# The new projection together with gate and up products between the routing steps, and the router on four column tiles

## The reference

```python
x = x + tanh(g_xattn[0]) * xattn(layernorm(x), ctx, ctx, Wq, bq, Wk, bk, Wv, bv, Wo, bo)   # 16 heads of 16
x = x + tanh(g_ffn[0]) * ffn(layernorm(x), w_router, fc1_w, fc2_w, gate_w, up_w, down_w)

def ffn(h, ...):                                  # h: 2048 x 256
    logits = h @ w_router                         # 256 x 8
    top_logits, top_idx = top_k(logits, 2)
    scores = softmax(top_logits)
    # each token goes through its two experts e:
    proj, gate = split(h @ fc1_w[e], 2)           # 256 x 512
    out_e = silu(proj) * gate @ fc2_w[e]          # 256 x 256
    moe = sum over the two experts of out_e * score
    shared = silu(h @ gate_w) * (h @ up_w) @ down_w   # 256 x 512, 512 x 256
    return moe + shared
```

## Time and profile before

| | |
|---|---|
| time, median of 3 runs | 496.63 us (495.54 to 497.8) |
| time of the profiled execution | 495.35 us |
| its span | 493.6 us, 7811 instructions |
| PE busy | 479.7 us, 97% of the span |
| DVE busy | 318.9 us, 65% |
| ACT busy | 228.9 us, 46% |
| POOL busy | 121.9 us, 25% |
| mean DMA rate | 112 GB/s |

### The profile page before, as it was taken

One profiled execution on the slowest core, in us unless ns is written; L12 is line 12 of the kernel. 1 busy time (PEld: TensorE's weight loads), 2 busy tenths in 40 slices (PEclk: granted clock), 3 DMA queues, 4 the chain that ended last, 5 costly groups with the idle time before them and its releaser, 6 DMA issues.

```text
span 493.6 us, 7811 instructions
## 1 busy us (share of the span) xinstructions
PE 479.7 (97%) x2234; PEld 245.9 (50%) x2235; DVE 318.9 (65%) x775; ACT 228.9 (46%) x487; POOL 121.9 (25%) x139
## 2 busy tenths in 40 slices
PE   8999898999999999999999999999999999999997
PEld 7555332332333323333457666565666666665645
DVE  1887887888888888888567776233333333332574
ACT  2655466777777777777754110032222333321010
POOL 5593483000000000000000757601333333333000
PEclk9999989999999999999999899999999999999999
DMA  8659742799994222220000213512222222221931
GB/s 257 201 176 252 160 152 76 192 194 190 196 191 143 66 65 67 64 66 1 3 2 0 76 64 108 183 38 71 86 89 91 87 85 85 87 74 45 329 122 60
DMA packets 49170, 55.46 MB, mean 112 GB/s; under 512 B 8080, under 2 KB 41232, under 8 KB 49136
## 3 DMA queue, kind: packets, MB, share of 16 engines
q1 hardware_dynamic: 44096, 43.86, 33.6%
q0 software_dynamic: 3408, 9.34, 5.4%
q10 hardware_dynamic: 1632, 1.84, 1.2%
HBM read 35.18 MB, written 19.71 MB: 111 GB/s over the span
## 4 chain that ended last, share of the span: by engine, by line
PE 84%; DMA 6%; DVE 4%; SPq 2%; ACT 1%; issue 1%; POOL 1%; ACTq 0%; POOLq 0%
PE PS L1420 14%; PE PS L1164 11%; PE PS L1331 11%; PE PS L1074 10%; PE PS L1282 10%; PE PS L1409 7%; PE PS L1343 6%; PE PS L1125 3%; PE PS L1212 2%; DMA R<-mparts 2%; PE PS L1174 2%; DMA X<-in_x_dram 2%; DMA q_parts<-R 2%; PE PS L1401 2%; PE PS L1394 2%; PE PS L1233 1%
## 5 line engine op out<-in xcount | busy, mean ns | idle before, releaser
L691 DVE TENSOR_REDUCE nmax<-PS 128x1 f32<-128x512 f32 x256 | 162.1, 682 | 18.5 <-PE PS L1074 17.9
L599 ACT ACTIVATE R<-PS 128x512 f32<-128x512 f32 x256 | 133.7, 603 | 41.9 <-PE PS L1282 41.8
L1074 PE MATMUL PS<-R 96*128 96x512 bf16 x256 | 96.5, 384 | 2.4 <-DMA R<-k_parts 1.6
L1282 PE MATMUL PS<-R 98*128 98x512 bf16 x256 | 86.3, 381 | 3.5 <-DMA R<-mparts 2.4
L1420 PE MATMUL PS<-R 128*128 x156 | 73.6, 594 | 1.5 <-ACT R L651 1.0
L1164 PE MATMUL PS<-R 128*32 128x512 f32 x512 | 68.2, 605 | 0.0
L487 POOL DMA_INDIRECT token_y<-R,dest x39 | 37.4, 959 | 98.9 <-DVE R L983 98.6
L999 DVE TENSOR_TENSOR R<-R,PS 128x256 f32<-128x256 f32 x39 | 16.4, 422 | 67.8 <-ACT R L648 42.2
L1074 PEld LDWEIGHTS PS<-R 96*128 96x128 bf16 x256 | 24.8, 97 | 58.2 <-DVE nmax L691 39.5
L648 ACT ACTIVATE R<-PS 128x256 f32<-128x256 f32 x39 | 15.0, 383 | 80.3 <-PE PS L1420 80.3
L463 POOL TENSOR_TENSOR rstd<-var_eps,minus_half 128x4 f32<-128x4 f32 x4 | 4.1, 1022 | 194.6 <-DVE var_eps L674 194.6
(11 more groups left out here) (135 smaller groups left out, 541.8 us busy)
## 6 DMA issues: line engine op xcount, KB each, us to landing
R<-q_parts SPq DMA_DIRECT2D x96, 64.0 KB, 3.1
R<-k_parts SPq DMA_DIRECT2D x96, 64.0 KB, 3.1
R<-slot_x SPq DMA_DIRECT2D x39, 129.0 KB, 2.1
R<-in_fc_w_dram SPq DMA_DIRECT2D x8, 512.0 KB, 4.2
R<-token_y SPq DMA_DIRECT2D x4, 1024.0 KB, 8.8
k_parts<-R SPq DMA_DIRECT2D x8, 384.0 KB, 3.1
q_parts<-R SPq DMA_DIRECT2D x8, 384.0 KB, 3.5
fc<-in_fc_w_dram SPq DMA_DIRECT2D x8, 256.0 KB, 5.3
```

The lines of the kernel that those rows point to most:

```text
L599: nc.scalar.activation(PT[:, kt, j, :], PS[:, (G * (TB * i + kt) + j) % 3, :], ACT.Exp).then_inc(exp_done, 1)
L691: nc.vector.tensor_reduce(nmax[:, i % 2, j * TB + qt:j * TB + qt + 1], PS[:, smax_bank(n), :], AX.X, ALU.max, negate=True).then_inc(max_re ...
L1074: mm(PS[:, smax_bank(n), :], QS[g][0:KS, j, qt * P:(qt + 1) * P], KST[g][0:KS, j, :], start=True, stop=True).then_inc(smax_done, 1)
L1282: mm(PS[:, n % 3, :], KST[g][0:KM, j, kt * P:(kt + 1) * P], QS[g][0:KM, j, :], start=True, stop=True).then_inc(st_done, 1)
```

## The change

The router product changes its sides. Before, 128 tokens were the stationary side and the 8 columns of `wr` the moving one. Now `wr` is the stationary side, padded with zeros to 32 columns (a memset on POOL, for which SP waits before it loads the weights), and the 128 tokens of `H2T` move; each of the four token tiles of a batch has its own column tile of the array. The logits come out turned (experts down, tokens across), in the first 128 columns of the bank. DVE copies them to `LT` (`logits_turned`), PE turns them (`router_rows`) into the next 128 columns, and DVE copies from there to `LG` as before.

The orders of PE, DVE, ACT and POOL in part 3 change with it: `gate_up(0, 0)` stands ahead of `router(1)`, each further piece of the shared expert stands one step earlier, between the router or the transposition and what follows it, and only one, `gate_up(1, 3)`, is left behind `down(0)`. POOL issues the first four scatters of batch 1 ahead of the `rstd` of batch 3.

```diff
-        wr = sb("wr", [P, DC, E])
+        wr = sb("wr", [P, DC, 32])
+        LT = sb("LT", [P, 2, P])
...
+                    sp.wait_ge(wr_zero, 1)
+                    sp.dma_start(wr[:, :, 0:E], w_router.rearrange("(c p) n -> p c n", p=P)).then_inc(w_in["router"], 16)
...
+            nc.gpsimd.memset(wr[:, :, :], 0.0).then_inc(wr_zero, 1)
...
             for b in range(B - 1):
                 rstd_second(b)
             scatter(0)
+            scatter(1, (0, 1))
             rstd_second(B - 1)
-            for b in range(1, B):
+            scatter(1, (2, 3))
+            for b in range(2, B):
                 scatter(b)
...
             h2t_first(1)
+            silu(0, 0)
             ctt_first(3)
-            silu(0, 0)
+            silu(0, 1)
             h2t_first(2)
-            silu(0, 1)
-            h2t_first(3)
             silu(0, 2)
             silu(0, 3)
+            h2t_first(3)
...
+            def logits_turned(b):
+                dve.wait_ge(lt_done, b + 1)
+                if b >= 2:
+                    dve.wait_ge(lg_done, b - 1)
+                nc.vector.tensor_copy(LT[:, b % 2, :], PS[:, bank("router", b), 0:P]).then_inc(lt_ready, 1)
...
                 for t in range(TB):
                     for c in range(DC):
-                        last = mm(PS[:, bank("router", b), t * E:(t + 1) * E], H2T[:, c, b * S + t * P:b * S + (t + 1) * P], wr[:, c, :],
-                                  start=(c == 0), stop=(c == DC - 1))
-                last.then_inc(lg_done, 1)
+                        last = mm(PS[32 * t:32 * (t + 1), bank("router", b), 0:P], wr[:, c, :],
+                                  H2T[:, c, b * S + t * P:b * S + (t + 1) * P],
+                                  start=(c == 0), stop=(c == DC - 1), tile_position=(0, 32 * t))
+                last.then_inc(lt_done, 1)
+
+            def router_rows(b):
+                pe.wait_ge(lt_ready, b + 1)
+                nc.tensor.transpose(PS[:, bank("router", b), P:2 * P], LT[:, b % 2, :], ident[:, :]).then_inc(lg_done, 1)
...
                     router(0)
-                    out_projection(2)
+                    out_projection(2, (0,))
+                    router_rows(0)
+                    out_projection(2, (1,))
```

More of the change, by code:

```diff
@@ L190, in flamingo_layer @@
         ctt_ready, h2t_ready = sems("ctt_ready", DC), sems("h2t_ready", DC)
+        wr_zero, lt_done, lt_ready = sem("wr_zero"), sem("lt_done"), sem("lt_ready")
         tg_bo_ready, x_biased = sem("tg_bo_ready"), sem("x_biased")
@@ L339, in _ @@
                         sp.dma_start(t_[:, :, :], src.rearrange("(c p) n -> p c n", p=P)).then_inc(w_in["shared"], 16)
-                    sp.dma_start(wr[:, :, :], w_router.rearrange("(c p) n -> p c n", p=P)).then_inc(w_in["router"], 16)
+                    sp.wait_ge(wr_zero, 1)
+                    sp.dma_start(wr[:, :, 0:E], w_router.rearrange("(c p) n -> p c n", p=P)).then_inc(w_in["router"], 16)
                 if 2 <= i < 2 + E // 2:
@@ L463, in rstd_second, with scatter @@
                 nc.gpsimd.tensor_tensor(rstd[:, sl], var_eps[:, sl], minus_half[:, sl], ALU.pow).then_inc(ln_rstd, 1)
-            def scatter(b):
+            def scatter(b, tiles=(0, 1, 2, 3)):
                 pool.wait_ge(tokens_in, 2)
                 pool.wait_ge(placed, b + 1)
-                for t in range(b * TB, (b + 1) * TB):
+                for t in (b * TB + n for n in tiles):
                     for k in range(2):
@@ L804, in logits @@
                 nc.vector.tensor_copy(LG[:, b * TB:(b + 1) * TB, :],
-                                      PS[:, bank("router", b), 0:TB * E].rearrange("p (t e) -> p t e", t=TB)).then_inc(lg_ready, 1)
+                                      PS[:, bank("router", b), P:2 * P].rearrange("p (t w) -> p t w", t=TB)[:, :, 0:E])\
+                    .then_inc(lg_ready, 1)
+            def logits_turned(b):
[3 more added lines that the diff above has]
+                nc.vector.tensor_copy(LT[:, b % 2, :], PS[:, bank("router", b), 0:P]).then_inc(lt_ready, 1)
             def hidden(b, c):
@@ L907, in tail @@
                 if n == 5:
+                    logits_turned(0)
                     logits(0)
@@ L939, in _ @@
             normalised(2)
+            hidden(0, 0)
+            logits_turned(1)
             logits(1)
@@ L942, in _ @@
             ctt_second(3)
-            hidden(0, 0)
             place(1)
+            hidden(0, 1)
             residual(3)
@@ L948, in _ @@
             normalised(3)
-            hidden(0, 1)
+            logits_turned(2)
+            hidden(0, 2)
             logits(2)
+            choose(2)
             h2t_second(3)
-            choose(2)
-            hidden(0, 2)
+            hidden(0, 3)
             place(2)
+            logits_turned(3)
+            hidden(1, 0)
             logits(3)
@@ L957, in _ @@
             nc.vector.tensor_tensor(sc[:, 0, :], mx8[:, :, 1], mx8[:, :, 0], ALU.subtract).then_inc(gap_ready, 1)
-            hidden(0, 3)
             place(3)
+            hidden(1, 1)
             tabulate()
-            hidden(1, 0)
+            hidden(1, 2)
             for h in range(2):
                 shared_out(0, h)
-            for b in range(1, BE):
-                for c in range(1 if b == 1 else 0, IC):
-                    hidden(b, c)
-                for h in range(2):
-                    shared_out(b, h)
+            hidden(1, 3)
+            for h in range(2):
+                shared_out(1, h)
             dve.wait_ge(exp_sc, 1)
@@ L1202, in ctx_transpose, with out_projection @@
                     last.then_inc(ct_t, 1)
-            def out_projection(b):
+            def out_projection(b, halves=(0, 1)):
                 pe.wait_ge(w_in["o"], 16)
@@ L1207, in out_projection @@
                     pe.wait_ge(ctt_ready[c], b + 1)
-                for h in range(2):
+                for h in halves:
                     bank_free("wo", b, h)
@@ L1311, in _ @@
             out_transpose(GROUPS - 1)
-            router(1)
             def gate_up(b, c):
@@ L1352, in count @@
                 mm(PS[:, bank("count", 0), 0:E], ones[:, :], PRE[:, NT, :], start=True, stop=True).then_inc(counted, 1)
+            assert BE == 2 and IC == 4
+            gate_up(0, 0)
+            router(1)
             ctx_transpose(3)
-            gate_up(0, 0)
+            router_rows(1)
+            gate_up(0, 1)
             rank(1)
@@ L1358, in _ @@
             h2_transpose(2)
-            gate_up(0, 1)
+            gate_up(0, 2)
             router(2)
+            gate_up(0, 3)
+            router_rows(2)
             h2_transpose(3)
-            gate_up(0, 2)
+            gate_up(1, 0)
             rank(2)
             router(3)
-            gate_up(0, 3)
+            router_rows(3)
+            gate_up(1, 1)
             rank(3)
-            gate_up(1, 0)
+            gate_up(1, 2)
             count()
             down(0)
-            for b in range(1, BE):
-                if b > 1:
-                    gate_up(b, 0)
-                for c in range(1, IC):
-                    gate_up(b, c)
-                    if c == 1 and b > 1:
-                        down(b - 1)
+            gate_up(1, 3)
             pe.wait_ge(w_in["fc1"], 16 * DC * E // 2)
```

## The result

| | median | range | runs |
|---|---|---|---|
| before | 495.81 us | 492.86 to 500.48 | 20 |
| after | 490.53 us | 488.83 to 496.22 | 20 |

The ratio is 0.9895, with a 95% interval of 0.9869 to 0.9922: 5.2 us less, between 3.9 and 6.5. The profiled execution took 489.82 us (span 488.0). Forecast were 492.8 us, range 491.2 to 495.6. Later comparisons showed more: on two further chips the changed kernel gained 4.4 and 5.1 us, on one it lost 2.6.

The account below looks back on a forecast made before the run. PE, busy 97% of the span, was taken as the bound. Routers -3.92, old waits -1.12, half-rate stretch -1.7 and new waits +3.53 gave -3.2 us: 492.1 profiled, 493.4 on the median, 492.8 forecast, range 491.2 to 495.6.

Parts of the forecast that it names:

- walk: From the router of batch 0 to the first expert transposes, each start the latest of what it awaits: -3.2 us.
- routers and turned rows: Four routers on PE, 6.96 us before, become 4 x 0.76 us with the added transposition: -3.92 us.
- old waits: PE's idling of 0.96 us before the router of batch 1 and 0.16 before `rank(2)` goes: -1.12 us.
- clock: PE's 3.41 us at granted clock 0.50 from 274.56 us goes, if none takes its place: -1.7 us.
- new waits: PE waits for DVE around `h2_transpose(1)`, `rank(0)`, batches 1 and 3, `gate_up(1,1)` and the last output projection: +3.53 us.
- change of tiling: Draining the engine at a router's new tiling mode costs at most the 0.14 us seen at L1164.
- rival 2: Router tiles start strictly in program order: 1.53 us a router, 493.9 us or 495.2 on the median; chance 0.18.
- rival 3: Router tiles do not overlap: 1.93 us a router, about 495.5 us, no gain; chance 0.08.
- rival 1: One half-rate stretch remains on PE: 493.8 us, or 495.1 on the median; chance 0.22.
- rival 4: Each of three light passages on PE draws a half-rate stretch, 5.1 us: 497.2 us, slower than before; chance 0.05.
- light passages: PE at 268.5 to 271.2, 274.7 to 277.1 and 297.4 to 300.2 us, with 1.0, 0.86 and 1.6 us idle.
- The expert rows: Their loads are in at about 323.8 us, PE asks at 325.5: hidden, with 1.7 us of cover.

Follow-up runs that it names:

- w3_order: New orders of all engines and the new buffers, with the old router product, against the kernel before on chip 7: 493.82 us against 496.44, ratio 0.9951.

## Why the prediction was right or wrong

Rows of PE from start to start give each term as it came out in the first two traces (walk: the prediction's way through the changed part). Three rows of the kernel before that the table needs and that are not shown so far, from its timeline of PE: the last context turn of the attention (`out_transpose`), and the two rows of `gate_up(0, 0)`, the first of them at half clock.

```profile
270.76 0.63 PE L1174 MATMUL PS<-ident,R 128*128 128x128 f32 x4
...
275.49 3.12 PE L1331 MATMUL PS<-R,wgate 128*128 128x512 f32 x4
278.45 1.88 PE L1331 MATMUL PS<-R,wup 128*128 128x512 f32 x4
```

| term | forecast | measured | from |
|---|---|---|---|
| routers and turned rows | -3.92 | -4.16 | 6.98 us of routers before; 4 x 0.595 + 4 x 0.11 after |
| old waits | -1.12 | -1.56 | `out_transpose` and wait 1.60 to 0.47, `rank(2)` and the product ahead of it 0.43 |
| clock | -1.7 | -1.72 | context transposes 1.35 to 0.87, first row of `gate_up` 2.96 to 1.72 |
| new waits | +3.53 | +3.44 | `h2_transpose(1)` 1.06, `LT` of batch 1 0.58, `out_projection(3)` 0.41, `LT` of batch 3 0.81, `gate_up(1, 1)` 0.58 |
| change of tiling, and the product behind a router | 0 | +0.4 | 0.10 ahead of three routers, 0.10 behind that of batch 2 |
| sum | -3.2 | -3.6 | passage -3.57 |

**The routers**: right, 0.60 us for 0.65 assumed. Rivals 2 and 3 (1.53 and 1.93 us) are refuted by that row, rival 2 again by the loop the other way round. For this shape the Trainium skill's sentence that matmuls start and end in program order ("TensorE: Matmul & The Clock Gate", Packing small matmuls) doesn't describe what the time shows: 0.60 us with the tiles outermost in the program, not 1.53.

**The waits**: right in place and releaser. The sum is right too, but by errors that cancel: 0.41 us ahead of `out_projection(3)` for 0.05 expected, against 0.58 for 0.86 at `LT` of batch 1, 0.81 for 0.9 and 0.58 for 0.72 at batch 3. The rows show only 0.54, 0.30, 0.24, 0.73 and 0.37 us of idling, 2.18 in all, and the term is still 3.44, since a pipeline that stops also loses the tail of the last matmul (0.66 us of a row whose successor would otherwise come after 0.44). The same holds for the old waits: the idling of 1.12 us that I took from the rows cost 1.56. I had sized the new waits by their signals and the old ones by their idling. That is 0.4 us more gain than I counted, and the change of tiling takes as much back; what is left of the walk's error is the routers' and, in small parts, the others'.

**The clock**: right, no stretch at 0.50 in any of the three passages of the changed kernel on quiet chips, and one in both of before there. The kernel before on chip 5 had none behind that router, so the 1.7 us are not certain in every execution. Rivals 1 and 4 did not come about on quiet chips. On chip 5 two such stretches came, behind waits of 5 us, not behind the light passages that rival 4 names.

**The change of tiling**: I had counted it inside the burst alone. The product ahead of a router takes 1.81 us (271.06 to 272.87), where ahead of the old router it takes 1.72 (`w3_order`, 285.53 to 287.25): entering costs some 0.1 us. The one behind takes 1.82, but behind the old router too it takes 1.80 (`w3_order`, 288.95 to 290.75), so leaving costs 0.02; the rest of that 0.10 is the price of a large product behind small ones, which the new order brings and not the tiles.

**The expert rows**: hidden as forecast, but with 0.4 us of cover. Counted from the first router, PE asks 0.3 us sooner than forecast (62.0 against 62.4), and the loads are issued 1.2 us later (59.35 against 58.2): they went out 3.25 us behind the last issue of zero rows, where the forecast had 2.3.

**What failed** is the last step of the sum, from the walk to the median, and the range around it. The prediction took the walk's -3.2 us as the gain of a whole execution; the medians gained 5.2. From its 492.8 us down to the measured 490.53 are 2.3 us. Of these, 0.2 are the start (496.0, the middle between the profiled execution and the median of three, where the median of twenty is 495.81) and 0.4 the walk. The other 1.7 us are gain beyond the passage, for which the sum had no term. Three comparisons on quiet chips give 5.2, 5.1 and 4.4 us, 4.9 on average, where the passages of the two kernels (two traces and three) differ by 3.6. Two of the three intervals hold 3.6 us, the first one ends at 3.9. Where the 1.3 us between 4.9 and 3.6 arise stays open: no trace shows them. The executions without a trace may have more stretches at half clock in the kernel before; the time ahead of the first router, which moves by 5.5 us between traces, may differ between the kernels (the layout, tried alone on chips 3 and 8 only, is not excluded by its intervals); or it is chance. The range's lower end came from changes of two terms of the walk only; it should have held the spread of the medians too.

And the sign is not one of the kernel alone. No step of the prediction spoke of the chip; on chip 5 the same kernel loses 2.6 us with signals that come 2 to 8 us late.

## What to carry to other kernels

Shortening an operation pays only where nothing else is awaited at once: the tiled router saved PE 4.2 us of work, but no gain showed in the old order, and 0.8 us of passage once large products stood ahead of the places at which PE waited for DVE. The order itself brought 2.8. Size a wait from the start of one row to the start of the next, not by its idle time, and put a large product of another stage between a short product and whoever needs its result. A gain of 1% that one chip shows should be tried on others before it is believed.

## What was not expected of the hardware

Four column tiles with 32 columns of weights each and 128 moving float32 columns run side by side: 16 records in 0.60 us from the first start to the next row's, the first four starting within 0.04 us, where 16 products one after the other took 1.70. Entering this shape cost some 0.1 us on the full product ahead of it, leaving it 0.02.

On three of the five chips whose number is known, signals of PE reached ACT and DVE 2 to 8 us (2.0, 6.4 and 7.7 in the trace of chip 5) after the matmul's modelled end, at places that depend on the order of PE's instructions and are the same from chip to chip; the kernel before takes 504 us there and 496 to 497 on the other two.
